# Rows rotated on their way out of PSUM, a scaled minimum in one instruction, and two small steps moved to ScalarE

## The reference

```python
s_i = relu(einsum('bthd,bsd->bths', q_i, k_i))      # 4 index heads
I = einsum('bths,h->bts', s_i, idx_w)
I = where(local, inf, I); I = where(causal, -inf, I)
_, idx = top_k(I, 96)                               # 64 local keys and 32 picked ones
...
key_r = _pope(kr_sel, angles_k)                     # picked keys rotated by their rank
scores = (q_c . k_c + q_r . key_r) * scale
attn = softmax(scores); out = attn . v;  return out @ W_out
```

## Time and profile before

| | us |
|---|---|
| median of 3 runs | 1138.89 |
| the three runs | 1138.05, 1138.89, 1146.54 |
| the profiled execution, its own time | 1145.09 |
| its span, first to last instruction | 1143.1 |
| busy in it: PE, DVE, ACT, POOL | 982.3, 816.7, 684.6, 588.5 |

### The profile page before, as it was taken

How to read it: one execution, slowest core, us unless ns; L and a number is a source line. 1 busy time by engine, 2 the same in 40 slices (tenths; PEclk the granted TensorE clock), 3 DMA queues, 4 the chain that set the end, 5 groups by cost and what they waited for, 6 DMA issues and landing times. The chain is left out here.

```text
span 1143.1 us, 19761 instructions
## 1 busy us (share of the span) xinstructions
PE 982.3 (86%) x6714; PEld 723.2 (63%) x6714; DVE 816.7 (71%) x1752; ACT 684.6 (60%) x1761; POOL 588.5 (51%) x616
## 2 busy tenths in 40 slices
PE   6999999998989884897898878888989787879786
PEld 4888877665658433565665667666766676567443
DVE  3777874746464578979888889978798989633237
ACT  3666645645454653766667658865686676655345
POOL 2100023424243077767777777777777777775000
PEclk8999999998999865958688778988788988887689
DMA  7100001000000068233433243313322333231000
GB/s 235 41 1 1 1 1 42 1 1 1 0 1 1 1 157 198 51 76 84 115 70 70 63 105 69 68 40 69 69 64 47 70 70 71 64 81 34 0 1 37
DMA packets 58626, 62.07 MB, mean 54 GB/s; under 512 B 27872, under 2 KB 43168, under 8 KB 58016
## 3 DMA queue, kind: packets, MB, share of 16 engines
q1 hardware_dynamic: 42656, 36.41, 12.5%
q0 software_dynamic: 15872, 24.41, 10.2%
HBM read 52.65 MB, written 8.13 MB: 53 GB/s over the span
## 5 line engine op out<-in xcount | busy, mean ns | idle before, releaser
L758 POOL DMA_INDIRECT gathered_rows<-key_table,idx_T x496 | 492.1, 992 | 182.5 <-issue 149.1
L773 PE MATMUL bank<-index_k_hi,index_q 128*128 128x512 f32 (+5 forms) x160 | 81.4, 511 | 24.5 <-ACT index_relu L1704 15.0
L1192 PE MATMUL bank<-ident,rotated_rows 128*96 128x128 f32 x512 | 92.2, 311 | 4.6 <-DVE rotated_rows L2254 4.6
L1721 ACT ACTIVATE turned_rows<-bank 96x512 f32<-96x512 f32 x128 | 74.2, 580 | 35.2 <-PE bank L1192 35.0
L2222 DVE SCALAR_TENSOR_TENSOR index_sums<-index_relu,iw,index_sums 128x512 f32<-128x512 f32 (+5 forms) x120 | 77.6, 647 | 21.3 <-ACT index_relu L1704 16.8
L1732 ACT ACTIVATE probs<-probs,attn_columns 128x208 f32<-128x208 f32 x128 | 59.5, 465 | 55.6 <-DVE attn_columns L2272 54.7
L1704 ACT ACTIVATE index_relu<-bank 128x512 f32<-128x512 f32 (+5 forms) x160 | 76.9, 496 | 23.8 <-PE bank L773 21.8
L2254 DVE TENSOR_TENSOR rotated_rows<-gathered_rows,rank_rope 128x384 f32<-128x384 f32 x128 | 71.0, 555 | 26.1 <-DMA gathered_rows<-key_table,idx_T 25.6
L1727 ACT ACTIVATE probs<-masked_scores,attn_columns 128x208 f32<-128x208 f32 x128 | 59.5, 465 | 34.8 <-DVE attn_columns L2267 27.8
L1216 PE MATMUL bank<-ident,probs 128*128 128x128 f32 x128 | 42.5, 332 | 43.9 <-ACT probs L1732 43.5
L2231 DVE MAX8 top<-index_sums 128x8 f32<-128x96 f32 (+15 forms) x64 | 78.2, 1222 | 1.2
(11 more groups left out here) (279 smaller groups left out, 2538.5 us busy)
## 6 DMA issues: line engine op xcount, KB each, us to landing
queries_in<-q_rot SPq DMA_DIRECT2D x32, 256.0 KB, 4.2
gathered_rows<-key_table,idx_T POOLq DMA_INDIRECT x496, 2.5
q_rot<-rotated SPq DMA_DIRECT2D x16, 256.0 KB
queries_in<-q_lat SPq DMA_DIRECT2D x16, 256.0 KB, 5.3
h<-in_h SPq DMA_DIRECT2D x2, 1024.0 KB, 7.6
q_lat<-q_latent_sb SPq DMA_DIRECT2D x8, 256.0 KB, 3.3
local_values<-key_table SPq DMA_DIRECT2D x15, 80.0 KB
x<-in_xT SPq DMA_DIRECT2D x1, 1024.0 KB, 5.2
```

Of the source, the lines that this page charges most:

```text
L758: pool.indirect_dma_start(out=G[b][:, q, :], out_offset=None, in_=key_table[0:index_width(i), :], in_offset=bass.IndirectOffsetOnAxis(ap=i ...
L773: return pe.matmul(out_, lhsT, rhs, start=start, stop=stop, **kw)
L1192: last = pe.transpose(bank[2][0:ROW, j * P:(j + 1) * P], GR[n % 2][:, j, :], ident[:])
L1721: fn(GT[n % 2], bank[2][0:ROW, :], ACT.Copy).then_inc(a_gts, 1)
```

## The change

The rotation moves behind the transposes. PE turns the gathered rows as they are; DVE multiplies the turned rows with a turned table while it takes them out of PSUM into SBUF, in place of ACT's copy. The rotated rows' own buffers go. In a slot DVE now does rows_rotate(n+1), after PE's rows_turn(n+1), where it did rows_rotate(n+2); PE waits for the gather itself.

The masked scores are computed with the factor -SCALE, so that a running minimum takes the place of the maximum and the small scaling instruction goes; exp takes them with the factor -1 and the minimum as bias. The sum of probabilities is inverted by ACT, as exp(-ln(sum)), just before it norms them. The first index head's product with its weight is computed by ACT out of the ReLU buffer; DVE adds the three others.

```diff
-    t["rank_rope"] = np.tile(row, (P // JG, 1)).astype(f32)
+    t["rank_rope"] = np.ascontiguousarray(np.tile(row, (P // JG, 1)).T).astype(f32)
...
+        def heads_added(u):
+            return u - (u + NIH - 1) // NIH
...
             def rows_turn(n):
-                pe.wait_ge(a_rot, n + 1)
+                i, g = n // NG, n % NG
+                if n < FIXED // GQ:
+                    pe.wait_ge(fixed_rows, 16 * QD)
+                else:
+                    gathers = i // 2 + (i % 2 == 1 or g >= FIXED // GQ)
+                    pe.wait_ge(gathered[i % 2][g], 16 * GQ // QD * gathers)
                 if n >= 1:
                     pe.wait_ge(a_gts, n)
                 for j in range(4):
-                    last = pe.transpose(bank[2][0:ROW, j * P:(j + 1) * P], GR[n % 2][:, j, :], ident[:])
+                    last = pe.transpose(bank[2][0:ROW, j * P:(j + 1) * P], G[i % 2][:, 4 * g + j, :], ident[:])
...
-                if u >= 4:
-                    act.wait_ge(i_used, u - 3)
-                fn(relu[:, u % 4, 0:w], bank[6 + u % 2][:, 0:w], ACT.Relu).then_inc(i_relu, 1)
+                if h > 0 and u >= NIH:
+                    act.wait_ge(i_used, heads_added(u - NIH + 1))
+                fn(relu[:, h, 0:w], bank[6 + u % 2][:, 0:w], ACT.Relu).then_inc(i_relu, 1)
+                if h == 0:
+                    if s0 == 0 and i >= 2:
+                        act.wait_ge(i_done, i - 1)
+                    act.wait_ge(i_relu, u + 1)
+                    fn(I_s[:, i % 2, s0:s0 + w], relu[:, 0, 0:w], ACT.Copy, scale=iw[:, 0:1]).then_inc(i_first, 1)
...
-            def rows_copy(n):
-                act.wait_ge(a_gt, n + 1)
-                if n >= 2:
-                    act.wait_ge(a_s, n - 1)
-                fn(GT[n % 2], bank[2][0:ROW, :], ACT.Copy).then_inc(a_gts, 1)
...
-                fn(Pr[n % 2], Sm[n % 2], ACT.Exp, scale=SCALE, bias=nb[:, n % 2:n % 2 + 1],
+                fn(Pr[n % 2], Sm[n % 2], ACT.Exp, scale=-1.0, bias=least[:, n % 2:n % 2 + 1],
                    accum_out=ssum[:, n % 2:n % 2 + 1]).then_inc(a_exp_s, 1)

             def probs_norm(n):
+                b = n % 2
+                act.wait_ge(a_exp_s, n + 1)
+                steps.did(fn(rsum[:, b:b + 1], ssum[:, b:b + 1], ACT.Ln))
+                fn(rsum[:, b:b + 1], rsum[:, b:b + 1], ACT.Exp, scale=-1.0).then_inc(a_rsum, 1)
                 act.wait_ge(a_rsum, n + 1)
                 fn(Pr[n % 2], Pr[n % 2], ACT.Copy, scale=rsum[:, n % 2:n % 2 + 1]).then_inc(a_pn, 1)
...
             def rows_rotate(n):
-                i, g = n // NG, n % NG
-                if n < FIXED // GQ:
-                    dve.wait_ge(fixed_rows, 16 * QD)
-                else:
-                    gathers = i // 2 + (i % 2 == 1 or g >= FIXED // GQ)
-                    dve.wait_ge(gathered[i % 2][g], 16 * GQ // QD * gathers)
+                dve.wait_ge(a_gt, n + 1)
                 if n >= 2:
-                    dve.wait_ge(a_gt, n - 1)
-                v.tensor_tensor(GR[n % 2], G[i % 2][:, 4 * g:4 * g + 4, :],
-                                rank_rope[:].unsqueeze(1).to_broadcast([P, 4, ROW]), ALU.mult).then_inc(a_rot, 1)
+                    dve.wait_ge(a_s, n - 1)
+                v.tensor_tensor(GT[n % 2].rearrange("r (j p) -> r j p", j=4), bank[2][0:ROW, :].rearrange("r (j p) -> r j p", j=4),
+                                rank_rope[:].unsqueeze(1).to_broadcast([ROW, 4, P]), ALU.mult).then_inc(a_gts, 1)
...
-                steps.did(v.tensor_tensor_reduce(out=Sm[b], in0=score_bank(n)[:, 0:KEYS], in1=mask[:], scale=1.0,
-                                                 scalar=LOWEST, op0=ALU.add, op1=ALU.max,
-                                                 accum_out=mx[:, b:b + 1]))
-                v.tensor_scalar(nb[:, b:b + 1], mx[:, b:b + 1], -SCALE, None, ALU.mult).then_inc(a_max, 1)
-
-            def sum_invert(n):
-                b = n % 2
-                dve.wait_ge(a_exp_s, n + 1)
-                v.reciprocal(rsum[:, b:b + 1], ssum[:, b:b + 1]).then_inc(a_rsum, 1)
+                v.tensor_tensor_reduce(out=Sm[b], in0=score_bank(n)[:, 0:KEYS], in1=mask[:], scale=-SCALE,
+                                       scalar=-LOWEST, op0=ALU.add, op1=ALU.min, accum_out=least[:, b:b + 1])\
+                    .then_inc(a_max, 1)
...
-                    if 0 <= n + 2 < GROUPS:
-                        rows_rotate(n + 2)
-                    if 0 <= n - 1 < GROUPS:
-                        sum_invert(n - 1)
+                    if 0 <= n + 1 < GROUPS:
+                        rows_rotate(n + 1)
```

More of the change, by code:

```diff
@@ L283, in hybrid_kernel @@
         QG = over("q_picked", [NG, P], parts=ROW)
-        GR = [over(f"rotated_rows{b}", [4, ROW]) for b in range(2)]
         GT = [over(f"turned_rows{b}", [C], parts=ROW) for b in range(2)]
@@ L287, in hybrid_kernel @@
         small = over("attn_columns", [8])
-        mx, nb, ssum, rsum = (small[:, 2 * k:2 * k + 2] for k in range(4))
+        least, ssum, rsum = (small[:, 2 * k:2 * k + 2] for k in range(3))
         assert at[0] <= SSM_END
@@ L392, in hybrid_kernel @@
             sem("topk_" + n + "_stored") for n in ("keys", "latents", "window_queries", "picked_queries"))
-        (i_s, i_relu, i_used, i_done, i_perm, i_idx) = (
-            sem("index_" + n) for n in ("scores", "relu", "relu_used", "picked", "permuted", "ready"))
+        (i_s, i_relu, i_first, i_used, i_done, i_perm, i_idx) = (
+            sem("index_" + n) for n in ("scores", "relu", "first_head", "head_added", "picked", "permuted", "ready"))
         fixed_rows = sem("fixed_rows")
@@ L398, in hybrid_kernel @@
         v_loaded = [sem(f"local_values_loaded{b}") for b in range(2)]
-        (a_rot, a_gt, a_gts, a_s, a_max, a_exp_s, a_pt, a_pts, a_pv, a_rsum, a_pn, a_otc, a_y, a_x) = (
+        (a_gt, a_gts, a_s, a_max, a_exp_s, a_pt, a_pts, a_pv, a_rsum, a_pn, a_otc, a_y, a_x) = (
             sem("attn_" + n) for n in (
-                "rows_rotated", "rows_turned", "rows_turned_copied", "scores", "max", "probs", "probs_turned",
+                "rows_turned", "rows_rotated", "scores", "max", "probs", "probs_turned",
                 "probs_copied", "values", "sum_inverted", "probs_normed", "out_copied", "projected",
@@ L1752, in topk @@
                     n = s - ATTN_LAG
-                    if 0 <= n + 1 < GROUPS:
-                        rows_copy(n + 1)
                     if 0 <= n - 1 < GROUPS:
@@ L2215, in pick @@
                     u = UNITS_BEFORE[i] + k
+                    if h == 0:
+                        return
                     dve.wait_ge(i_relu, u + 1)
-                    r_, s_ = relu[:, u % 4, 0:w], sc[:, s0:s0 + w]
-                    if h == 0:
-                        ins = v.tensor_scalar(s_, r_, iw[:, 0:1], None, ALU.mult)
-                    else:
-                        dve.wait_ge(i_used, u)
-                        ins = v.scalar_tensor_tensor(s_, r_, iw[:, h:h + 1], s_, ALU.mult, ALU.add)
-                    ins.then_inc(i_used, 1)
+                    if h == 1:
+                        dve.wait_ge(i_first, u // NIH + 1)
+                    else:
+                        dve.wait_ge(i_used, heads_added(u))
+                    r_, s_ = relu[:, h, 0:w], sc[:, s0:s0 + w]
+                    v.scalar_tensor_tensor(s_, r_, iw[:, h:h + 1], s_, ALU.mult, ALU.add).then_inc(i_used, 1)
                 elif what == "mask":
-                    dve.wait_ge(i_used, UNITS_BEFORE[i + 1])
+                    dve.wait_ge(i_used, heads_added(UNITS_BEFORE[i + 1]))
                     if i == 0:
```

## The result

The changed kernel takes 1131.21 us (median of 21 runs, 1128.02 to 1139.29), the kernel before, measured beside it, 1146.54 (21 runs, 1137.41 to 1155.37 but for one of 3525.44, which the median does not feel). The ratio is 0.990, with a 95% interval of 0.988 to 0.992. The medians are 15.3 us apart. The profiled execution took 1129.24 us, its span 1127.2: 15.9 us less than that of before, where 12.6 were forecast.

The account below looks back on a forecast made before the run. The gathers were taken as the stage's bound. Attention -4, locks -7.4, front +0.3 and end -1.5 sum to -12.6 us; off the median 1138.89 that gives 1126 us, range 1118 to 1137, each with 4 us more.

Parts of the forecast that it names:

- The bound: Gather stage, 402.55 to 1050.88 us: 496 gathers at 1.25 us each make 620 of 648.3 us the floor.
- three long waits: POOL waiting for attention's buffers: waits of 3.89, 1.46 and 0.94 us, costing 5.4 us over the ordinary 0.30.
- (1) The rotation: DVE's rotation reading PSUM: +0.13 us a group on DVE, 45 long gathers become short, -7.4 us.
- second rival: The PSUM rotation holds gathers like the old one, or something else did: 1133 us; chance 0.13.
- (2) to (5): First head, reciprocal to ACT, turned-row copy off ACT, scaled minimum: DVE sheds 17.7 us by the head, ACT +13 us.
- wait for an older pick: ACT's first-head copy waits 14 times for the pick two tiles before: taken as nothing, bound 1 us each.
- (6) The order: DVE's rotation of n+1 behind PE's transposes of n+1: attention gains 4 us before 553.5, bounds 7 to a loss.
- full gain: Attention runs ahead: the full 6.9 us before 553.5 and 3 at the end, 17 us: 1122 us; chance 0.12.
- the locks: Gathers held by the rotation and first head's product, shed after 553.5 us: 6.4 + 1.0 = 7.4 us.
- the end: After the last gather lands, PE's transposes of group 127 start earlier: -1.5 us, bounds 0 and -3.
- The front: ACT's chain to the table of keys, before the gathers, gets one more copy between two ReLUs: +0.3 us.
- third rival: DVE's wait for PE's transposes costs attention 1.2 us a slot in 22 slots before 553.5: 1156 us; chance 0.07.

Follow-up runs that it names:

- extra_sbuf: Changed kernel plus an unused 96 by 512 DVE product, both inputs in SBUF, ahead of every rotation; ratio to before 1.0344.
- extra_psum: Changed kernel plus the same unused DVE product ahead of every rotation, its first input read from PSUM; ratio to before 1.0283.
- rest_only: Kernel before with the scaled minimum, first head and inverted sum on ScalarE; old rotation and its ACT copy kept; ratio to before 0.9991.
- late_rotation: Changed kernel with DVE's rotation moved behind the row minimum of its slot; ratio to before 0.9976, on another chip 0.9977.
- after_again: The changed kernel once more, as control on another chip; ratio to before 1.0134.
- before_again: The kernel before, unchanged, for a trace on a slower chip; ratio to before 1.0026.

## Why the prediction was right, and where it was not

**The bound.** That the gathers set the stage is borne out on the chip of the result: 11.0 us of gather time and 5.4 us of waits are the whole shortening of the stream, and the spans differ by the stream, the front and the tail. It is an account of two traces, not an experiment, since none of the four other chips was bound by them. What the experiments show is that it was true of that chip and not of the kernel: on the others POOL waits 190 to 209 us for attention, and a shorter mean of the gathers (975 to 969 ns, 2.9 us in all) was worth nothing. One reading of the sum was off without harm: only two of the three long waits, 3.89 and 1.46 us, are among the eight for PE, of which six are ordinary; the profile gives the one of 0.94 us to "issue". The 5.4 us over the ordinary 0.30 stay.

**(1) The rotation.** Forecast 684 ns from the nearest row, measured 683. The 45 long gathers are gone with their 7.4 us, and extra_sbuf against extra_psum shows that the SBUF input was the cause. So the second rival is settled. The inference on the Trainium skill's page "SBUF — State Buffer", section "Who interferes with whom", that a tensor_tensor leaves descriptor generation alone, does not agree with these runs: the SBUF product takes a gather from 0.94 to 1.29 us. The rule of the same section on a second SBUF input does agree.

**(2) to (5) ScalarE's new work.** The copy of a head 722 ns (at most 700 were taken), the columns 199 and 203 ns each (205). The wait for an older pick, which I priced at nothing with 1 us each as the bound, occurred once and was 6.2 us, beyond that bound; it was hidden, for POOL had no long wait after it. rest_only shows these parts neutral where slots bound.

**(6) The order.** The forecast took 4 us from attention before 553.5 and named 6.9 as the full gain. All of it came: POOL has no wait left above 0.3 us, and group 8's values are 5.9 us earlier. This term was sized too small, by 2.9 us. Which part of the change made attention faster there was not isolated on that chip. Further 0.4 us came from fewer holds by the sums and 1.7 from fewer by the rotation of queries and other rows, which I had left as they were: together with the locks they make the stream's -16.4 against -11.4. The full gain that I gave 0.12 was thus the truth for the stage, but not at the end, where I had priced 1.5 and 1.0 came. PE's granted clock was 0.69 between 1000 and 1050 us, where before had 0.76: it spent more of the stretch at the lower of its two levels, 1.2 GHz. That this took the 0.5 us is not shown. The front gave 0.24 against 0.3.

The time itself, 1126, lies 5 us under the measured 1131 although the change gained 3 us more than forecast: I had subtracted from the median of three runs, 1138.89, and over 21 runs the kernel before has 1146.54. That the number came so near owes something to luck: a base 7.7 us too low and a gain 2.7 us too small (12.6 against 15.3) work against each other.

**The third rival.** It had the right mechanism at a wrong address. I looked at one pair of rows, PE at 488.43 and DVE at 489.56, and weighed it for 22 slots of one chip, where the wait came to 1.9 us. What failed in this step is that one pair of rows in one execution was taken as a property of the order. Already on the result's chip the wait grew to 79.6 us behind those slots, where the gathers hid it. On the other chips it is 211 us over 128 slots, each group takes 0.11 us longer than before's, and the change is 1.3% slower. The chance of 0.07 agrees with the outcome on the result's chip, and was far too low for a statement about the kernel.

**The version to keep.** late_rotation has all of the change's gains in the gathers (974 and 972 ns) and none of DVE's wait. Against the changed kernel's 1.0134 it gives 0.9976 and 0.9977, 1.6% less, set side by side across chips; against before its intervals just reach 1. On a chip like the result's it was not run; there POOL's waits were already at their least in the changed kernel, so I would expect no difference, but none is shown.

## What to carry to other kernels

Where an order of slots hands work from one engine to another within the same slot, put the receiver's instruction behind work that it can do meanwhile. The wait at the head cost nothing visible here while the gathers were the bound, and 1.2% of the time once the slots were. Before such an edit is called good, measure on more than one chip, and ask of each trace anew which engine the others wait for. Compare the pace of each of the two candidates per group (here 5.2 us for four gathers against 4.76 or 6.35 us for a slot): it says which of them is likely to set the end. An indirect gather that meets a DVE product of two SBUF inputs is shortened by taking one of them from PSUM, and this can pay only where the gathers bound.

## What the runs showed of the hardware

The same program took 1146 us on one chip and 1353 to 1358 on four others. Up to the first gather they are within 9 us of one another (it starts at 402.6 us in after_again, 411.0 in before_again, 402.6 and 404.1 on the result's chip), and from the last group's values to the end it is 79 us in before and in before_again; all but 8 of the 216 us between these two come in the stage of slots, 6.35 us a group against 4.76, with a granted clock of 0.73 against 0.83. Each chip was used at one time only, so that the chip itself makes the difference is likely and not shown. The changed kernel's rotation waits for PE alone, and on the slower chips about half of this wait lies behind the recorded end of PE's instruction (103 of 211 us in after_again, none on the result's chip). A clock that is low because PE stands and a PE that is late because the clock is low would look the same here, and telling them apart would take a run in which PE's work per slot is changed alone.

A held gather ends 0.81 to 0.82 us after the DVE instruction that holds it, whichever that is: this is the median over the held gathers in every trace gone through, and extra_sbuf's pair above has 533.50 + 1.29 - 533.28 - 0.69 = 0.82. It was seen behind products and sums of two SBUF inputs (the old rotation, the rotation of queries, the sum of heads, the unused product), and at the same length behind one form with a single SBUF input and its output in SBUF, the first head's product, here in the trace of before:

```profile
452.60 0.49 DVE L2219 TENSOR_SCALAR index_sums<-index_relu,iw 128x512 f32<-128x512 f32 x1
452.70 1.21 POOL L758 DMA_INDIRECT gathered_rows<-key_table,idx_T  x1 [0.30 <-issue]
```

So two SBUF inputs are not the whole rule. MAX8, FIND_INDEX8 and MATCH_REPLACE8, which read and write SBUF as well, ran over the start of 131 gathers of before and held none (mean 944 ns), and in before and after no gather ended 0.82 us behind a DVE instruction that reads PSUM. DVE has to be there first: in these two traces the sum of heads and the first head's product held the gathers that they preceded by 0.10 us or more, and left at 0.94 us the 11 that they preceded by 0.02 to 0.09 us.
